# One index column copied and awaited ahead of each row gather, in place of sixteen for sixteen, in a mixture-of-experts kernel

## The reference

```
xn   = layernorm(x)
out  = x + attention(xn) + ffn(xn)
attention: 16 heads of 16, keys within 128 positions of the query, softmax, then a projection
ffn:       top 8 of 64 experts by sigmoid(xn @ router_w), their scores scaled to sum 1;
           sum over the eight of w_e * (silu(xn @ gate_e) * (xn @ up_e)) @ down_e,
           plus a shared expert that every token visits
```

## Time and profile before

| what | us |
|---|---|
| median of three runs | 1383.55 |
| the profiled execution's own time | 1376.39 |
| its span, first to last instruction | 1374.3 |
| part one | 0 to 226 |
| the expert part | 226 to 846 |
| attention and the rest | 846 to 1374.3 |
| PE busy over the span | 1163.8 (85%) |
| DVE / ACT / POOL busy | 778.3 / 728.1 / 635.7 |

### The profile page before, as it was taken

One profiled execution on the slowest core, in us unless ns is written; L12 is line 12 of the kernel. 1 busy time (PEld: TensorE's weight loads), 2 busy tenths in 40 slices (PEclk: granted clock), 3 DMA queues, 4 the chain that ended last, 5 costly groups with the idle time before them and its releaser, 6 DMA issues. The chain is left out here.

```text
span 1374.3 us, 33994 instructions
## 1 busy us (share of the span) xinstructions
PE 1163.8 (85%) x8297; PEld 806.2 (59%) x8298; DVE 778.3 (57%) x2491; ACT 728.1 (53%) x1914; POOL 635.7 (46%) x658
## 2 busy tenths in 40 slices
PE   6988895799988989998989888788887878878779
PEld 3544564677777778777877775344443434444347
DVE  7776795233433333343333336777777777777743
ACT  3554574465655555555555554455545555554553
POOL 1344013455554555554545554555555555655530
PEclk9999898899999999999999998899999999999999
DMA  6888203576666776666755563354445455444413
GB/s 221 221 211 226 93 1 133 150 201 217 190 206 199 203 219 207 197 197 208 207 165 176 156 175 118 97 138 117 119 118 135 116 127 129 118 119 114 113 44 123
DMA packets 142996, 213.79 MB, mean 156 GB/s; under 512 B 19425, under 2 KB 115682, under 8 KB 142946
## 3 DMA queue, kind: packets, MB, share of 16 engines
q0 software_dynamic: 27648, 86.02, 23.0%
q1 hardware_dynamic: 70946, 84.42, 22.6%
q10 hardware_dynamic: 44352, 42.74, 9.1%
HBM read 142.59 MB, written 70.26 MB: 155 GB/s over the span
## 5 line engine op out<-in xcount | busy, mean ns | idle before, releaser
L1030 POOL DMA_INDIRECT xb<-token_rows,idx_ring_x x320 | 304.1, 950 | 291.1 <-DVE ys L1157 212.5
L1647 POOL DMA_INDIRECT yg<-expert_rows,idx_ring x256 | 266.5, 1041 | 207.9 <-PE psum L1356 120.0
L1058 PE MATMUL psum<-xTe,wb_and_xT_all_or_onorm 128*128 128x128 f32 x2560 | 350.2, 280 | 14.1 <-ACT wb_and_xT_all_or_onorm L1107 8.1
L1477 ACT ACTIVATE pT<-psum 128x384 f32<-128x384 f32 (+1 forms) x512 | 211.5, 467 | 242.6 <-PE psum L1356 225.1
L1058 PEld LDWEIGHTS psum<-xTe,wb_and_xT_all_or_onorm 128*128 128x128 f32 x2560 | 314.0, 193 | 31.8 <-ACT wb_and_xT_all_or_onorm L1107 18.2
L1157 DVE TENSOR_SCALAR ys<-psum,xb 128x256 f32<-128x256 f32 x320 | 154.6, 483 | 312.7 <-PE psum L1067 277.5
L1542 DVE CUSTOM_DVE_ANT_0 masked<-psum,mask_q 128x384 f32<-128x384 f32 (+1 forms) x512 | 247.4, 519 | 85.4 <-PE psum L1363 78.3
L1067 PE MATMUL psum<-wb_and_xT_all_or_onorm,aT 128*128 x640 | 198.5, 392 | 32.2 <-DVE ys L1157 23.9
L1093 ACT COPY xTe<-psum 128x256 f32<-128x256 f32 x320 | 119.1, 372 | 193.3 <-PE psum L1048 130.9
L1371 PE MATMUL psum<-qk 98*128 98x384 bf16 (+1 forms) x512 | 168.6, 331 | 54.2 <-ACT pT L1477 49.1
L1107 ACT COPY wb_and_xT_all_or_onorm<-wb_and_xT_all_or_onorm 128x512 f32 x320 | 200.0, 626 | 17.7 <-SPq L995 4.8
(11 more groups left out here) (134 smaller groups left out, 1103.2 us busy)
## 6 DMA issues: line engine op xcount, KB each, us to landing
expert_rows<-ys ACTq DMA_DIRECT2D x160, 256.0 KB
wb_and_xT_all_or_onorm<-in_w_exp SPq DMA_DIRECT2D x64, 384.0 KB
qk<-q_stacks SPq DMA_DIRECT2D x32, 384.0 KB
q_stacks<-wb_and_xT_all_or_onorm SPq DMA_DIRECT2D x32, 192.0 KB, 2.7
qk<-k_parts SPq DMA_DIRECT2D x32, 192.0 KB
k_parts<-wb_and_xT_all_or_onorm SPq DMA_DIRECT2D x28, 192.0 KB, 3.0
token_rows<-rows SPq DMA_DIRECT2D x8, 640.0 KB, 4.4
xb<-token_rows,idx_ring_x POOLq DMA_INDIRECT x320
```

The lines of the kernel that those rows point to most:

```text
L1030: nc.gpsimd.indirect_dma_start(out=xb[:, r, :], out_offset=None, in_=rows_d, in_offset=bass.IndirectOffsetOnAxis(ap=idx_ring[:, q, r:r + 1 ...
L1058: last = nc.tensor.matmul(banks[GU + r % NB][:, part * P:(part + 1) * P], wgu[:, r % NW, h, part * I:(part + 1) * I], xT[:, r % NX, h, :], ...
L1477: nc.scalar.activation(pT[:, (j % 2) * HG + hh, 0:(hi - lo) * P], key_bank(j, hh)[:, 0:(hi - lo) * P], ACT.Exp).then_inc(p_ready, 1)
L1647: nc.gpsimd.indirect_dma_start(out=yg[:, h, k, :], out_offset=None, in_=y_d, in_offset=bass.IndirectOffsetOnAxis(ap=idx_ring[:, h, k:k + 1 ...
```

## The change

Inside `step(i, q)`, the wait ahead of the copy, the copy of sixteen columns and the one wait for it go. In their place, ahead of each of the sixteen gathers, POOL copies the one column that this gather reads to the same place in `idx_ring` and waits for that copy; the semaphore `idx_ready` now counts blocks. The wait for `ys_ready` and the raising of `tick` ahead of each gather are as before, and now stand behind the copy and its wait. Nothing else is changed: ACT copies the weights at L1107 in both kernels.

```diff
             def step(i, q):
-                if not first(i) or q > 1:
-                    pool.wait_ge(ys_ready, i * (2 * XR) + (q - 1) * XR)
-                    pool.sem_inc(tick, 1)
-                nc.gpsimd.tensor_copy(idx_ring[:, q, :], slot_ids[:, bass.ds(i * (2 * XR) + q * XR, XR)]
-                                      ).then_inc(idx_ready, 1)
-                pool.wait_ge(idx_ready, i * 2 + q + 1)
                 for r in range(XR):
+                    at = i * (2 * XR) + (q * XR + r)
+                    nc.gpsimd.tensor_copy(idx_ring[:, q, r:r + 1], slot_ids[:, bass.ds(at, 1)]).then_inc(idx_ready, 1)
+                    pool.wait_ge(idx_ready, at + 1)
                     if not first(i) or q > 0:
                         pool.wait_ge(ys_ready, i * (2 * XR) + (q * XR + r - XR + 1))
                         pool.sem_inc(tick, 1)
```

## The result

The changed kernel takes 1417.98 us, the median of four runs (1413.55 to 1421.46), against 1381.25 us for the kernel before on the same chip. The ratio is 1.027 with a 95% interval of 1.0221 to 1.0318: slower by 37 us, where 37 us had been forecast. The profiled execution took 1421.46 us.

The account below looks back on a forecast made before the run. PE was taken to bound the kernel at 1.883 us per block; the change makes POOL the bound at 2.03 us. The last turning moves from 837.57 to 874.8 us, +37.3 us on the median 1383.55: 1421 us, range 1397 to 1447 us.

Parts of the forecast that it names:

- The 0.87 us are a floor and not a wait for DVE: POOL's idle time from a copy's end to the next gather in the loop: 0.87 us, the cost of copy wait and start.
- The copy takes 0.175 us: One-column copy on POOL ahead of each gather: 0.175 us, the middle between 0.147 and 0.205 us.
- the slope that I took from a copy on one partition: Copy length on POOL: 3.9 ns per column from a 96-element copy of 0.514 us, giving 0.147 us for one column.
- The first step's period is 1.77 us: POOL's first sixteen gathers, with constants and no buffer wait: 0.98 + 0.175 + 0.61 = 1.77 us each.
- The loop's period is 2.03 us: POOL's shortest period for the loop's 288 gathers: 0.98 + 0.175 + 0.87 = 2.03 us, adding 584.6 us.
- The second step's period is 1.95 us: POOL's second sixteen gathers, waiting for buffers by constants: 1.95 us each, with 0.79 us from wait to gather.
- 5 us from a gather to its turning: Last block of the expert part: turned some 5 us after gather 319 starts at 869.8 us, so at 874.8 us.
- PE busy 83% of the part: PE in the expert part: busy some 1.69 of each 2.03 us, 83%; a 5% clock loss would vanish in spare time.
- POOL's fill was covered: POOL's fill behind the last gather: ends near 877.8 us, covered by PE and DVE until about 882, 4 us to spare.
- PE sets the pace at 1.883 us with small losses: Expert part before the change: PE is the bound, gathers follow it at 1.883 us per block, POOL has 0.63 us slack.
- The rival "faster": Expert part: a steady POOL pace removes PE's losses; at 1.77 us per block 34 us are won, 1350 us; chance 0.03.
- Slack takes it: POOL's loop: 0.61 us is the true cost behind a copy, period 1.77 us, hidden by the 16-buffer lead: 1384 us; chance 0.13.

Follow-up runs that it names:

- the written-out kernel: The changed kernel with POOL's twenty steps written out instead of looped, so all wait values are constants: 1404.92 us, ratio 1.0201.
- The experiment on the order: Changed kernel with steps written out, and the copy and its wait moved behind the wait for the buffer and the tick: 1379.27 us, ratio 1.0018.
- the one with a second copy: The changed kernel with a second one-column copy, to a spare tile, ahead of the awaited one: 1446.9 us, ratio 1.0505.
- the one with half rows: The changed kernel gathering 160 numbers per row in place of 320: 1320.09 us; the same edit to the kernel before: 1173.26 us.
- four or seven unawaited copies: Kernel before with four or seven one-column copies to a spare tile ahead of each gather, awaited only at the part's end: 1318.16 and 1427.13 us.
- the kernel with one fill: The kernel before with one unawaited fill of 240 columns in a spare tile ahead of each gather: 1171.05 us, ratio 1.0004.

## Why the prediction was right

The step on which all rested held: POOL's own shortest period, found from the rows around 20 old copies, rose over the pace at which blocks were consumed, and the absolute times of the gathers then gave the end. The last turning was forecast at 874.8 us and came at 874.57. Point by point:

- *The 0.87 us are a floor and not a wait for DVE.* Right: 0.86 or 0.82 us behind every copy of the loop. In half of the steps (q = 1) no register operation stands between the two waits, hence 0.82, as in the written-out kernel. The experiment on the order says what the floor is: the stop of the stream, not the copy's round trip.
- *The copy takes 0.175 us.* It takes 0.193:

```profile
L1022 POOL COPY idx_ring_x<-tokens_of_slots x320: 185/193/196, 226.1 to 870.2; 128x1 int32 x144, 128x1 int32<-128x1 int32 x16
```

  Fifteen columns fewer save 0.013 us from 0.206. This is what the estimate by the rule of the Trainium skill (GPSIMD Engine Reference, Performance versus the Vector engine) had given, some 0.19 us; the slope that I took from a copy on one partition was wrong. It makes 0.018 x 319 = 6 us.
- *The first step's period is 1.77 us.* It is 1.45: 0.27 us behind a copy, and the 0.61 of the earlier trace rows belongs to the first gather only (0.62 again). I took the one sample for the rule. From 228.56 to 248.88 us fifteen gathers start, so 14 x 0.32 = 4.5 us less than forecast.

```profile
226.90 1.18 POOL L1027 DMA_INDIRECT xb<-token_rows,idx_ring_x  x1 [0.62 <-POOL idx_ring_x L1022]
228.10 0.19 POOL L1022 COPY idx_ring_x<-tokens_of_slots 128x1 int32<-128x1 int32 x1
228.56 0.98 POOL L1027 DMA_INDIRECT xb<-token_rows,idx_ring_x  x1 [0.27 <-POOL idx_ring_x L1022]
```

- *The loop's period is 2.03 us.* It is 2.00 or 2.05 in nearly all rows and 2.05 on average (871.24 - 282.88, over 287). Three pauses of some 2.4 us each, at 445, 646 and 847 us, and nine short ones are in the mean; nothing in my sum stood for them, and the three alone are 7 us. The first is in the rows above. They belong to the count of gathers and not to the time: they come ahead of gathers 113, 211 and 309, each 98 after the last, in the written-out kernel, in the one with a second copy and in the one with half rows too, on three chips. With four or seven unawaited copies only the one ahead of gather 113 is left. Their cause stays open.
- *The second step's period is 1.95 us.* It is 2.00 us, 0.8 us over its sixteen gathers.
- *5 us from a gather to its turning.* 3.3 us. The forecast had the first step 5.1 us too long, the second 0.8 us and the loop 5.8 us too short, and the turning 1.7 us too long, and these cancel to 0.2 us. The sum was right by its mechanism and luckier than its terms.
- *PE busy 83% of the part.* 546.30 / 657 = 83%. The granted clock was 0.99 over the part: it fell to the lower level (1.2 GHz) for 3.4 us at 453.8 and again at 655.2 us, a few us behind the first two of the three pauses. POOL's fill was covered.

What was wrong without harm is the sentence that PE sets the pace at 1.883 us with small losses. PE can do a block in 1.55 us; the rest was lost on the chips where the results of PE are seen late. The sum didn't need the reason, since it was made from gather 0 to gather 319 in absolute times. But it took the time before, 837.57 us for the last turning, as it was on this chip, and so the 37 us hold for such a chip only: with half rows the change cost 147 us on the third. The rival "faster" did use it, and was nearer to the truth than its chance of 0.03 says in one respect: a steady pace of POOL below 1.88 us does take the late results away, as four unawaited copies show (1.71 us, 60 us won). Its condition, that POOL's period be under 1.883, wasn't met, as the prediction said. "Slack takes it" is what happens when the order of the waits is changed.

## What to carry to other kernels

An awaited result ahead of a DMA costs little (0.27 us here) when its wait is the last thing ahead of the DMA, and the whole time of handing over the DMA (0.82 us) when another wait with a semaphore operation stands between and the result isn't there yet. Compare the shortest period of an engine with the pace of the work it feeds, not its busy share: POOL was 51% busy before and 58% after, and yet 0.17 us per block too slow. Where PE paces a kernel, look whether the time is the same on another chip; POOL's period, 2.05 and 2.04 us on average, was the same on both chips that showed it.

## What the runs showed of the hardware that wasn't expected

The same kernel takes 1377.7 and 1375.9 us on two chips and 1170.5 us on two others. The first part takes 226 us on all. The rest differs: in the kernel with one fill, on the third chip, the expert part takes 509 us (226 to 735) against 620 us in the kernel before on the chip of the profile, with blocks at 1.546 against 1.88 us, and 435 us follow it against 528 us. The granted clock doesn't explain the expert part: it is 1.00 from 300 to 820 us before, and 1.00 from 300 to 700 us there. Behind the expert part it is 0.95 against 0.97, which by an estimate from these two figures accounts for some 10 us of the 94.

On the first two chips, adding work to POOL made the kernel faster, 1318 us at a shortest period of 1.67 us and 1331 us at 1.56 us. The version with four unawaited copies beats both kernels there; it wasn't run on the other two, where its period of 1.67 us lies over PE's 1.546. Shown is that the late results are gone where POOL alone sets the pace, at 1.67 us or more, and that a lead of ten buffers instead of sixteen doesn't end them. What makes them late on those chips, and whether PE needs pauses or the gathers a distance, stays open.

Copies of POOL that nobody awaits overlap: four of 0.193 us take 0.54 us, seven 0.89 us.
